# The experts' first product as three fp32r products of high and low parts, with the weights split at the head of the stage

## The reference

```python
xn = _layernorm(x)
logits = h @ router_weight.T + router_bias              # h = xn as 4096 rows of 256
top_vals, top_idx = jax.lax.top_k(logits, 2)
top_w = softmax(top_vals)                               # scores: top_w at top_idx, else 0
gate_up = einsum('th,ehj->etj', h, gate_up_proj) + gate_up_proj_bias[:, None, :]
gate = minimum(gate_up[..., ::2], 7.0)
up = clip(gate_up[..., 1::2], -7.0, 7.0)
act = (up + 1.0) * (gate * sigmoid(gate * 1.702))
expert_out = einsum('eti,eih->eth', act, down_proj) + down_proj_bias[:, None, :]
ffn = einsum('te,eth->th', scores, expert_out)          # g = silu(ffn)
```

## Time and profile before

| | |
|---|---|
| median of 3 runs | 1133.09 us (1131.99 to 1135.56) |
| the profiled execution | 1132.22 us |
| span of its trace | 1130.4 us |
| busy: PE, DVE, ACT, POOL | 941.0, 937.8, 777.8, 225.3 us |
| mean granted TensorE clock | 0.945 of full speed |
| experts' stage: first xs load issued, first `gate_and_up` | 768.86 us, 772.30 us |
| last y store issued in that stage | 1011.46 us |

### The profile page before, as it was taken

The page is one execution under the profiler, slowest core; times in us unless marked ns, Lnnn a source line. Parts: engine busy times, 40 slices in busy tenths (PEclk is TensorE's granted clock), DMA queues, the critical chain, the costliest instruction groups (busy, mean ns, idle before and its releaser), DMA issues. The chain is left out here.

```text
span 1130.4 us, 25744 instructions
## 1 busy us (share of the span) xinstructions
PE 941.0 (83%) x6626; PEld 657.1 (58%) x6627; DVE 937.8 (83%) x1872; ACT 777.8 (69%) x1982; POOL 225.3 (20%) x427
## 2 busy tenths in 40 slices
PE   5888875989889898998989989876999999962665
PEld 4666653666666666666666666653555555541544
DVE  6676757999999999999999999963777777764887
ACT  3444334999999999999999999972333333325563
POOL 2000000122223222232222322220000000007771
PEclk9999985999999999999999999997999999996677
DMA  7988967578676786766657566501222222223553
GB/s 274 353 318 304 329 256 202 126 179 197 165 178 154 178 194 164 178 156 138 152 120 165 129 140 151 118 20 50 80 79 83 83 80 79 84 82 104 163 179 118
DMA packets 92410, 178.11 MB, mean 158 GB/s; under 512 B 11744, under 2 KB 50144, under 8 KB 91360
## 3 DMA queue, kind: packets, MB, share of 16 engines
q1 hardware_dynamic: 74336, 147.38, 48.6%
q0 software_dynamic: 7680, 20.98, 6.3%
q10 hardware_dynamic: 10368, 9.44, 2.5%
HBM read 108.56 MB, written 69.21 MB: 157 GB/s over the span
## 5 line engine op out<-in xcount | busy, mean ns | idle before, releaser
L1032 DVE TENSOR_REDUCE nmax<-bank 128x1 f32<-128x1024 f32 (+3 forms) x256 | 259.9, 1015 | 4.2 <-PE bank L864 4.1
L965 ACT ACTIVATE Pr_long<-bank,nmax 128x1024 f32<-128x1024 f32 (+3 forms) x256 | 252.2, 985 | 10.9 <-DVE nmax L1032 10.8
L992 ACT COPY AT<-bank 128x512 f32<-128x512 f32 (+3 forms) x384 | 177.2, 494 | 3.8 <-PE bank L903 1.8
L862 PE MATMUL bank<-Ks_first,Qs_first 128*128 128x512 f32 (+3 forms) x384 | 124.2, 413 | 31.0 <-ACT Pr_short L979 19.8
L979 ACT ACTIVATE Pr_short<-bank,nmax 128x128 f32<-128x128 f32 (+3 forms) x256 | 138.4, 541 | 8.9 <-DVE nmax L1050 1.5
L1224 PE MATMUL bank<-gu_sb,xsT 128*128 x288 | 140.1, 610 | 4.7 <-DVE hid L1341 0.5
L903 PE MATMUL bank<-ident,Pr_long 128*128 128x128 f32 x832 | 127.4, 280 | 18.0 <-DVE Pr_long L1082 17.9
L1082 DVE SCALAR_TENSOR_TENSOR Pr_long<-Pr_long,coef 128x1024 f32<-128x1024 f32 (+3 forms) x128 | 137.4, 1074 | 0.0
L862 PE MATMUL bank<-Ks_second,Qs_second 128*128 128x512 f32 (+3 forms) x384 | 119.5, 400 | 19.8 <-ACT Pr_short L979 19.5
L864 PE MATMUL bank<-maskb,identb 128*128 128x128 bf16 x512 | 118.2, 233 | 0.0
L926 PE MATMUL bank<-AT,Vj 128*32 128x128 f32 x2304 | 108.7, 278 | 0.0
(11 more groups left out here) (147 smaller groups left out, 1633.4 us busy)
## 6 DMA issues: line engine op xcount, KB each, us to landing
q_parts<-PARTS SPq DMA_DIRECT2D x32, 512.0 KB, 3.7
k_parts<-PARTS SPq DMA_DIRECT2D x32, 512.0 KB, 3.7
Qs_first<-q_parts SPq DMA_DIRECT2D x64, 256.0 KB
Ks_first<-k_parts SPq DMA_DIRECT2D x64, 256.0 KB
Qs_second<-q_parts SPq DMA_DIRECT2D x64, 256.0 KB, 5.8
Ks_second<-k_parts SPq DMA_DIRECT2D x64, 256.0 KB, 6.8
xs_dram<-zeros SPq DMA_DIRECT2D x8, 1152.0 KB, 7.3
xs<-xs_dram SPq DMA_DIRECT2D x72, 128.0 KB, 2.0
```

Source lines behind the costliest of these rows:

```text
L862: nc.tensor.matmul(at[:, c0:c1], Qs[head][:, m, q * P:(q + 1) * P], Ks[head][:, m, c0:c1], start=True, stop=(c1 < N))
L965: nc.scalar.activation(long_probs(p)[:, m, 0:N], long_slot[m][:, 0:N], ACT.Exp, bias=nmax[:, 4 * p + m:4 * p + m + 1], scale=1.0, accum_ou ...
L992: nc.scalar.copy(AT[u % 6][:, 0:w], tb[u % BANKS][:, 0:w]).then_inc(unit_out, 1)
L1032: nc.vector.tensor_reduce(nmax[:, 4 * p + m:4 * p + m + 1], long_slot[m][:, 0:N], AX.X, ALU.max, negate=True).then_inc(long_maxed, 1)
```

## The change

The first product no longer uses fp32 matmuls on `xsT` and `gu_sb`. At the head of the stage ScalarE copies each expert's weights to `gu_high` (fp32r) and VectorE writes the rest to `gu_low`, eight instructions each of 128 x 1024 elements. For each tile ScalarE writes the high part of the turned rows where it wrote `xsT` before, and a new function `low_rows` on VectorE writes the low part; its place in the step is behind `gate(n+1)` and ahead of `output(n-1)`. `gate_and_up` has six fp32r matmuls in place of two fp32 ones and waits for the low part; the first one also waits until all weights are split. `glu` shares its buffer with `gate_tanh` and `act_in` with `up`, and two waits move accordingly.

```diff
-            xsT = [sb(f"xsT{u}", [P, HC, P], where=ph) for u in range(2)]
+            gu_high = sb("gu_high", [P, HC, E, 2 * I], F32R, where=ph)
+            gu_low = sb("gu_low", [P, HC, E, 2 * I], F32R, where=ph)
+            gu_parts = [gu_high[:], gu_low[:]]
+            xsT = [sb(f"xsT{u}", [P, 2, HC, P], F32R, where=ph) for u in range(2)]
-            glu = [sb(f"glu{u}", [P, I], where=ph) for u in range(2)]
+            glu = gate_tanh
-            act_in = [sb(f"act_in{u}", [P, I], where=ph) for u in range(2)]
+            act_in = up
...
# turn_rows, gate_and_up (TensorE)
-                    nc.tensor.wait_ge(xsT_ready, seen(it, u - 2))
+                    nc.tensor.wait_ge(xsT_lo, seen(it, u - 2))
...
-                    nc.tensor.wait_ge(xsT_ready, seen(it, u))
+                    nc.tensor.wait_ge(xsT_lo, seen(it, u))
                     nc.tensor.wait_ge(hid_ready, seen(it, u - 2))
-                    for c in range(HC):
-                        last = nc.tensor.matmul(hbank[u], xsT[u][:, c, :],
-                                                gu_sb[:, c, bass.ds(e, 1), :]...,
-                                                start=(c == 0), stop=(c == HC - 1))
+                    products = [(c, r, w) for c in range(HC) for r, w in ((0, 0), (0, 1), (1, 0))]
+                    for c, r, w in products:
+                        last = nc.tensor.matmul(hbank[u], xsT[u][:, r, c, :],
+                                                gu_parts[w][:, c, bass.ds(e, 1), :]...,
+                                                start=..., stop=...)
...
                     turn_rows(0, 1)
+                    pe.wait_ge(gu_lo, E)
                     load = expert_loader(pe)
...
# rows_out, gate_curve (ScalarE)
-                    nc.scalar.copy(xsT[u][:]..., xbank[u][:, 0:HC * P]).then_inc(xsT_ready, 1)
+                    nc.scalar.copy(xsT[u][:, 0]..., xbank[u][:, 0:HC * P]).then_inc(xsT_hi, 1)
...
-                    nc.scalar.wait_ge(glu_ready, seen(it, u - 2))
+                    nc.scalar.wait_ge(act_ready, seen(it, u - 2))
...
+                    act.wait_ge(ew_loaded, 64 * E)
+                    for e in range(E):
+                        nc.scalar.copy(gu_high[:, :, e, :], gu_sb[:, :, e, :]).then_inc(gu_hi, 1)
                     rows_out(0, 0)
...
# VectorE
+                def low_rows(it, n):
+                    it, u = it + n // 2, n % 2
+                    nc.vector.wait_ge(xsT_hi, seen(it, u))
+                    nc.vector.tensor_tensor(xsT[u][:, 1]..., xbank[u][:, 0:HC * P],
+                                            xsT[u][:, 0]....bitcast(F32), ALU.subtract).then_inc(xsT_lo, 1)
...
+                    nc.vector.wait_ge(act_turned, seen(it, u - 2))
                     nc.vector.tensor_scalar(up[u][:], hid[u][:, I:], LIMIT, -LIMIT, ALU.min, ALU.max)...
...
-                    nc.vector.wait_ge(act_turned, seen(it, u - 2))
...
+                    for e in range(E):
+                        dve.wait_ge(gu_hi, e + 1)
+                        nc.vector.tensor_tensor(gu_low[:, :, e, :], gu_sb[:, :, e, :],
+                                                gu_high[:, :, e, :].bitcast(F32), ALU.subtract).then_inc(gu_lo, 1)
+                    low_rows(0, 0)
+                    low_rows(0, 1)
                     load = expert_loader(dve)
...
                         gate(it, n + 1)
+                        low_rows(it, n + 2)
                         output(it, n - 1, e)
```

More of the change, by code:

```diff
@@ L1132, in build @@
             xs_turned = sem("xs_turned")
-            xsT_ready = sem("xsT_ready")
+            xsT_hi = sem("xsT_hi")
+            xsT_lo = sem("xsT_lo")
+            gu_hi = sem("gu_hi")
+            gu_lo = sem("gu_lo")
             hid_bank = sem("hid_bank")
@@ L1219, in gate_and_up @@
                     it, u = it + n // 2, n % 2
-                    nc.tensor.wait_ge(xsT_ready, seen(it, u))
+                    nc.tensor.wait_ge(xsT_lo, seen(it, u))
                     nc.tensor.wait_ge(hid_ready, seen(it, u - 2))
-                    for c in range(HC):
-                        last = nc.tensor.matmul(hbank[u], xsT[u][:, c, :],
-                                                gu_sb[:, c, bass.ds(e, 1), :].rearrange("p o n -> p (o n)"),
-                                                start=(c == 0), stop=(c == HC - 1))
+                    products = [(c, r, w) for c in range(HC) for r, w in ((0, 0), (0, 1), (1, 0))]
+                    for c, r, w in products:
+                        last = nc.tensor.matmul(hbank[u], xsT[u][:, r, c, :],
+                                                gu_parts[w][:, c, bass.ds(e, 1), :].rearrange("p o n -> p (o n)"),
+                                                start=((c, r, w) == products[0]), stop=((c, r, w) == products[-1]))
                     last.then_inc(hid_bank, 1)
@@ L1280, in rows_out @@
                     nc.scalar.wait_ge(hid_bank, seen(it, u - 2))
-                    nc.scalar.copy(xsT[u][:].rearrange("p c n -> p (c n)"), xbank[u][:, 0:HC * P]
-                                   ).then_inc(xsT_ready, 1)
+                    nc.scalar.copy(xsT[u][:, 0].rearrange("p c n -> p (c n)"), xbank[u][:, 0:HC * P]
+                                   ).then_inc(xsT_hi, 1)
                 def gate_curve(it, n):
@@ L1317, in _ @@
                         act.sem_inc(y_stored[u], 16)
-                    for s in (xsT_ready, tanh_ready, act_T_ready):
+                    for s in (xsT_hi, tanh_ready, act_T_ready):
                         act.sem_inc(s, 2)
+                    act.wait_ge(ew_loaded, 64 * E)
+                    for e in range(E):
+                        nc.scalar.copy(gu_high[:, :, e, :], gu_sb[:, :, e, :]).then_inc(gu_hi, 1)
                     rows_out(0, 0)
@@ L1343, in hidden @@
                                             ).then_inc(hid_ready, 1)
+                def low_rows(it, n):
+                    if not there(it, n):
+                        return
+                    it, u = it + n // 2, n % 2
+                    nc.vector.wait_ge(xsT_hi, seen(it, u))
+                    nc.vector.tensor_tensor(xsT[u][:, 1].rearrange("p c n -> p (c n)"), xbank[u][:, 0:HC * P],
+                                            xsT[u][:, 0].rearrange("p c n -> p (c n)").bitcast(F32), ALU.subtract
+                                            ).then_inc(xsT_lo, 1)
                 def gate(it, n):
@@ L1386, in _ @@
                 def _(dve):
-                    for s in (hid_ready, gate_ready, glu_ready, up_ready, act_ready, y_ready):
+                    for s in (xsT_lo, hid_ready, gate_ready, glu_ready, up_ready, act_ready, y_ready):
                         dve.sem_inc(s, 2)
+                    for e in range(E):
[4 more added lines that the diff above has]
+                    low_rows(0, 1)
                     load = expert_loader(dve)
```

## The result

The changed kernel takes 1148.81 us (median of 4 runs, 1147.68 to 1149.40), the kernel before beside it 1134.0 us (1131.99 to 1135.56): ratio 1.0127, 95% interval 1.0114 to 1.0140. It is slower by 14.8 us; forecast were 21, with a range of 1142 to 1167 us. The profiled execution took 1149.05 us with a span of 1147.2 us, 16.8 more than before.

A forecast was written before the change was run, and what follows sets the result against it. TensorE was taken to bound the kernel before, and a ring through low_rows the changed one. Profiled 1132.2 + 14 (ring) + 7.5 (head) = 1153.7 us, 1154.6 against the median, stated as 1154; range 1142 to 1167.

The forecast's parts named there:

- the ring: Experts' stage, every tile: low_rows, product, hidden, gate, low_rows wait on each other; 6.88 us a turn, +14 us.
- the lap: Once round low_rows, product, hidden, gate and back to low_rows: 3.44 us a tile, from 3.25 to 3.6.
- gate to `low_rows`: On VectorE, from gate's start to low_rows' start: 0.33 to 0.41 us, taken as 0.37.
- Product to reader: From the product's first matmul on TensorE to its first reader, hidden on VectorE: 1.87 us, lower bound 1.70.
- Hop to TensorE: From the end of low_rows on VectorE to the product's start on TensorE: about 0.05 us.
- the low end: Lower bound of a tile's lap: 3.25 us, with product to reader 1.70 and gate to low_rows 0.33.
- VectorE alone 6.55 to 6.96 us a turn, even the lower is above today's: VectorE's own work with low_rows added: 6.12 + 0.70 - 0.27 to 6.12 + 0.84 us, against today's 6.49.
- The step with the loop's work: VectorE's step holding the loop's own work: it overlaps low_rows, giving some 2.3 us instead of 2.62.
- rival 1: VectorE's loop work is not overlapped: that step 3.72 us, a turn 7.16, +24 us and the head, 1164; chance 0.27.
- The head: Start of the experts' stage: splitting the weights, 9.1 us of subtractions, delays the first product by 7.5 us, bounds 6 and 9.5.
- Rivals 3, 4 and 5: TensorE stays bound, 1116 us, chance 0.05; TensorE's clock drops, +70 us or more, 0.03; products further apart, 1172 us, 0.05.
- At nothing: Experts' stage: moved waits, shared buffers, output's later place and unchanged DMAs were claimed to cost nothing.

The follow-up runs named there:

- the last run: Against the changed kernel with low_rows ahead of gate and the up clip on GpSimd: two of eight experts' weights split by GpSimd; 1130.08 us, ratio 0.9967.

## Why the prediction was right

- **The bound and the mechanism** were right. TensorE lost its lead to a ring that closes through the new wait. Shown: the wait on each tile in the trace, and three runs that change the ring and nothing of VectorE's amount (`low_rows` later +38 us, product shorter -16, `low_rows` earlier -17), against one that changes VectorE's amount and not the ring (0 us).
- **The size of the lap** was 3.44 us, found 3.33, and so 14 us of the sum were 6.7, less than half: a lap 3% shorter takes away most of the small difference between two laps and the turn before. The forecast of the whole time is 5 us high mainly by this. Term by term: gate to `low_rows` 0.37 forecast, 0.21 found, the largest miss. I bounded it by two rows in which the follower was held: ys had waited for its product, and glu to up is a longer instruction's spacing. Product to reader 1.87, found 1.79. Hop to TensorE 0.05, found 0.23 and 0.14 behind the end of `low_rows` (901.20 to 901.43, 904.57 to 904.71): I took it from a hop to ScalarE. The first two errors outweigh the third. The lap's other terms were within 0.01. The bounds were added up carelessly: the terms of the low end give 3.23 and not 3.25, and those shown for the high end 3.48, so that 3.6 has no terms behind it.
- **"VectorE alone 6.55 to 6.96 us a turn, even the lower is above today's"** was wrong. Found at most 6.12 (a turn of the changed kernel, 6.66, less the 0.54 us of the marked wait) and about 6.11 by the run with four products; and with `low_rows` added to the kernel before no cost at all. The step that failed is the 6.12 to which I added the instruction: it held about 1 us of gaps, and I let only 0.27 of them absorb something.
- **The step with the loop's work.** I argued that this work would start while `low_rows` ran, and so the lap, not VectorE's path, would set that step. The lap does: with the clip gone VectorE waits 0.45 us there. But the argument was not the reason: ys to glu is still 0.90 us with 0.48 of "issue", hardly overlapped. VectorE's path was just short enough, because four of its five spacings are shorter than I took them: 0.33 + 0.90 + 0.34 + 0.39 + 0.34 = 2.30 where rival 1 had 0.42 + 0.96 + 0.33 + 0.49 + 0.42 = 2.62 (the last term found is that of the kernel with four products), against 0.65 + 1.79 = 2.44 for the ring's part. Right outcome, wrong reason, and so partly luck. The queue depth of 8 that the Trainium skill gives ("Advanced Engine Details and Errata", Engine Queue Depths) did not hide the loop's work in this trace: 0.48 us of "issue" stand ahead of glu.
- **The head** was 7.5, found 7.65 in the changed kernel and 7.66 alone. The 9.1 us for the eight subtractions came out at 9.17.
- **Rivals 3, 4 and 5** did not come: TensorE was not the bound; the clock stayed at 1.00 in the steady stretch at 17.70 of 20 us busy; the products follow 0.23 us apart but for the first two, 0.33 (901.43 to 901.76), so that the six take 1.48 us where I had 1.40.
- **At nothing**: the buffers and moved waits cost nothing (ratio 0.9999). The DMAs are the same.

## What to carry to other kernels

When a fast engine's input gets a new producer on a slow in-order engine, write down the ring: new producer, consumer, whatever the slow engine must still do behind the consumer's result until it comes to the producer again. Where its lap is longer than either engine's own work, the lap is the period; and its cure is the order in the slow engine's step, here one line moved and 17 us. An instruction put where an engine sat idle anyway can be free, and taken from there it can uncover another wait, as with the tanh. And a wait that the profile puts down to one engine is worth laying beside that engine's rows: a wait of 0.64 us named after the tanh here lasted 0.52 us beyond the tanh's end.

## What the hardware showed unexpectedly

- GpSimd and VectorE take turns. VectorE's subtraction of 128 x 1024 took 1.2 us alone; in the last run, beside GpSimd's two, the first took 1.75 and the next two 3.37 and 3.36. The single rows, cut from narrow windows:

```profile
771.14 1.04 POOL L1340 CAST gu_high<-gu_sb 128x1024 fp32r<-128x1024 f32 x1
771.50 1.75 DVE L1434 TENSOR_TENSOR gu_low<-gu_sb,gu_high 128x1024 fp32r<-128x1024 f32 x1 [15.08 <-ACT gu_high L1356]
772.14 3.31 POOL L1343 TENSOR_TENSOR gu_low<-gu_sb,gu_high 128x1024 fp32r<-128x1024 f32 x1
773.17 3.37 DVE L1434 TENSOR_TENSOR gu_low<-gu_sb,gu_high 128x1024 fp32r<-128x1024 f32 x1
775.42 3.32 POOL L1343 TENSOR_TENSOR gu_low<-gu_sb,gu_high 128x1024 fp32r<-128x1024 f32 x1
776.47 3.36 DVE L1434 TENSOR_TENSOR gu_low<-gu_sb,gu_high 128x1024 fp32r<-128x1024 f32 x1
```

Their ends alternate: 772.18 (GpSimd's copy), 773.25, 775.45, 776.54, 778.74, 779.83. Each of VectorE's ends 1.07 to 1.09 us behind the end of GpSimd's, each of GpSimd's 2.20 us behind the end of VectorE's, as if each began only when the other was done. The Trainium skill ("SBUF — State Buffer", "SBUF: two separate sides") says that the two share a port pair, held by one instruction to its end, and that a VectorE instruction with two SBUF inputs competes for it with a GpSimd one that reads SBUF. This trace agrees.
- VectorE's gate, 128 x 256 in SBUF, lasts 0.29 us, yet its successor starts 0.21 us behind its start.
- A group of six fp32r matmuls hands over 1.79 us behind its start, 0.4 us more than six spacings of 0.23; in a ring that latency is paid on each lap.
